# Four graph layers on one core: one-hots of the block build made column by column from one key a lane, and one f32 product for the weights

## The reference, cut to what matters

```python
edge_index = jnp.stack([src, dst])
h = jnp.maximum(_layernorm(x, axis=-1), 0.0)
x = x + _L0_gnn_ref(h, edge_index, ...)                        # message MLP with attention, 2 steps
h = jnp.maximum(_layernorm(x, axis=-1), 0.0)
x = x + _L1_gnn_ref(h, edge_weight, src, dst, ...)             # weighted means both ways, GRU
h = jnp.maximum(_layernorm(x, axis=-1), 0.0)
x = x + _L2_gnn_ref(h, edge_index, edge_attr_4, ...)           # 4 edge types, 4 GRU steps
h = jnp.maximum(_layernorm(x, axis=-1), 0.0)
x = x + _L3_gnn_ref(h, edge_index, edge_type_16, ...)          # 16 relations
```

```python
m = ft[src] * w[:, None]
msum = jax.ops.segment_sum(m, dst, num_segments=n_nodes)
wsum = jax.ops.segment_sum(w, dst, num_segments=n_nodes)
```

## Time and profile before

| | |
|---|---|
| Timed runs | 7994.43 us median of 3 (7987.53 to 8007.56) |
| Profiled execution | 8035.26 us, span of its instructions 8033.2 us |
| PE busy | 5862.3 us, 73% of the span |
| DVE busy | 3623.5 us, 45% |
| ACT busy | 1789.9 us, 22% |
| POOL busy | 2370.6 us, 30% |
| `decode` | from about 579.5 to 597 us |
| `build_blocks` | from about 597 to 1411 us |

### The profile page before, as it was taken

One profiled execution on the slowest core, in us unless ns is written; L12 is line 12 of the kernel. 1 busy time (PEld: TensorE's weight loads), 2 busy tenths in 40 slices (PEclk: granted clock), 3 DMA queues, 4 the chain that ended last, 5 costly groups with the idle time before them and its releaser, 6 DMA issues. The chain is left out here.

```text
span 8033.2 us, 101908 instructions
## 1 busy us (share of the span) xinstructions
PE 5862.3 (73%) x31333; PEld 4116.2 (51%) x31441; DVE 3623.5 (45%) x7508; ACT 1789.9 (22%) x4498; POOL 2370.6 (30%) x2471
## 2 busy tenths in 40 slices
PE   1437777566766676666668989899898997666665
PEld 1334444366666656666664444444444443566555
DVE  6889999355555545555556532221222214111111
ACT  1006666233333333333331010100101002000000
POOL 0000000355655535555550000000000000666665
PEclk8669999788888888888888999999999998555555
DMA  1005555333333423333335635355453543111111
GB/s 50 1 7 212 204 207 207 111 101 100 102 100 100 98 79 101 101 101 101 100 100 184 230 133 192 128 192 176 143 192 127 192 164 136 45 44 45 45 44 43
DMA packets 418900, 951.09 MB, mean 118 GB/s; under 512 B 61905, under 2 KB 274310, under 8 KB 408582
## 3 DMA queue, kind: packets, MB, share of 16 engines
q1 hardware_dynamic: 314502, 681.10, 24.9%
q0 software_dynamic: 104192, 267.02, 12.3%
HBM read 741.69 MB, written 206.20 MB: 118 GB/s over the span
## 5 line engine op out<-in xcount | busy, mean ns | idle before, releaser
L1516 POOL DMA_INDIRECT ring<-rows,stage x1632 | 1586.9, 972 | 2038.4 <-issue 1064.8
L1587 PE MATMUL ps<-here,spread 128*128 x3264 | 1098.7, 467 | 843.2 <-DVE ring L1546 576.8
L1166 PE MATMUL ps<-strip,trans_part 128*128 128x512 f16 (+1 forms) x8400 | 1645.4, 357 | 14.9 <-DVE trans_part L1127 14.9
L1406 POOL DMA_INDIRECT ring<-rows,stage x808 | 772.2, 956 | 2993.9 <-ACT stage L1390 2581.0
L1166 PEld LDWEIGHTS ps<-strip,trans_part 128*128 128x128 bf16 x8400 | 781.1, 98 | 930.6 <-issue 65.7
L1587 PEld LDWEIGHTS ps<-here,spread 128*128 128x128 f32 x3264 | 656.6, 223 | 967.2 <-issue 899.1
L1546 DVE TENSOR_TENSOR ring<-ring,ps 128x512 f32<-128x512 f32 x816 | 560.5, 687 | 1259.7 <-remote 611.3
L1444 PE MATMUL ps<-ring,mark 128*128 128x128 f32 x1616 | 627.0, 488 | 373.2 <-DMA ring<-rows,stage 242.4
L1605 PE MATMUL ps<-ring,mark 128*128 128x128 f32 x3264 | 772.4, 327 | 0.0
L1605 PEld LDWEIGHTS ps<-ring,mark 128*128 128x128 f32 x3264 | 648.9, 221 | 65.1
L1444 PEld LDWEIGHTS ps<-ring,mark 128*128 128x128 f32 x1616 | 433.4, 326 | 397.0 <-issue 397.0
(11 more groups left out here) (288 smaller groups left out, 6279.3 us busy)
## 6 DMA issues: line engine op xcount, KB each, us to landing
strip<-adj SPq DMA_DIRECT2D x400, 800.0 KB, 4.4
adj<-piece SPq DMA_DIRECT2D x125, 640.0 KB, 3.1
locs<-loc_rows SPq DMA_DIRECT2D x420, 128.0 KB
ahead<-ahead_piece SPq DMA_DIRECT2D x125, 320.0 KB, 2.2
back<-back_piece SPq DMA_DIRECT2D x125, 320.0 KB, 2.4
sheet<-ahead SPq DMA_DIRECT2D x25, 1600.0 KB, 8.7
sheet<-back SPq DMA_DIRECT2D x25, 1600.0 KB, 7.2
ring<-rows,stage POOLq DMA_INDIRECT x2440
```

The source lines that it names most:

```text
L1166: last = eng.matmul(k.ps[:, b, 0:cols], part[:, s % TABLES, m, t * D:(t + 1) * D], strip[:, n % RING, c0:c0 + cols], start=n == 0 and m == ...
L1406: eng.indirect_dma_start(ring[:, t, :], None, rows, bass.IndirectOffsetOnAxis(stage[:, t:t + 1], 0)).then_inc(s_full[q], 16)
L1516: eng.indirect_dma_start(ring[:, t, :], None, rows, bass.IndirectOffsetOnAxis(stage[:, t:t + 1], 0)).then_inc(s_full[q], 16)
L1587: last = eng.matmul(hid[:, j, :], spread[:, q, t * P:(t + 1) * P], here[:, bass.ds(cols[t] * 2, W2)], start=True, stop=True)
```

## The change

`decode` stores one number a lane and slot in f32: the new `lane_of` (source lane), `dst_of`, `pair_of`, and `weight_of`, the sum of the three weight parts, made by two additions. `src_of` stays as it was, and feeds `left`.

`build_blocks` makes `left` as before. `right` is made by ten tensor-scalar instructions, one a slot, that compare a row of 512 column numbers (f16) with one key a lane. `down` and `heavy` are f32 now and made slot by slot with 128 columns each: `down` compares with the destination lane, `heavy` compares with the source lane and multiplies by the weight, both read as one operand a lane. The order is `left`, all of `right`, then `down` and `heavy` in turn. TensorE makes the weighted blocks by two f32 products a block, where there were six in bf16. `s_hot` counts three steps a group.

```diff
--- before.py
+++ after.py
@@ -507,16 +507,15 @@
     k.back = nc.dram_tensor("back", [NP + 1, NP], F32, kind="Internal").ap()
     with ExitStack() as own:
 
-        src_of, dst_of = (k.sb(n, [P, BINS * 2, 2], BF16, own) for n in ("src_of", "dst_of"))
-        pair_of = k.sb("pair_of", [P, BINS * 2, 2], F16, own)
-        part_of = k.sb("part_of", [P, 3, BINS * 2, 2], BF16, own)
+        src_of = k.sb("src_of", [P, BINS * 2, 2], BF16, own)
+        lane_of, dst_of, pair_of, weight_of = (k.sb(n, [P, BINS * 2], F32, own) for n in ("lane_of", "dst_of", "pair_of", "weight_of"))
         with ExitStack() as inner:
             binned = k.sb("binned", [P, WORDS, NW, NW, 2], F32, inner)
             with ExitStack() as most:
                 sort_bins(k, most, binned)
-            decode(k, inner, binned, src_of, dst_of, pair_of, part_of)
+            decode(k, inner, binned, src_of, lane_of, dst_of, pair_of, weight_of)
         with ExitStack() as inner:
-            build_blocks(k, inner, src_of, dst_of, pair_of, part_of)
+            build_blocks(k, inner, src_of, lane_of, dst_of, pair_of, weight_of)
     k.edges.close()
     with ExitStack() as own:
         build_any(k, own)
@@ -680,7 +679,7 @@
     k.end_phase()
 
 
-def decode(k, own, binned, src_of, dst_of, pair_of, part_of):
+def decode(k, own, binned, src_of, lane_of, dst_of, pair_of, weight_of):
 
     first, second = (k.sb(n, [P, NW, NW, 2], I32, own) for n in ("first_word", "second_word"))
     whole = k.sb("whole", [P, NW, NW, 2], I32, own)
@@ -696,18 +695,20 @@
             c.step(eng.tensor_copy(flat(second), flat(binned[:, 1, :, :, :])))
             c.step(eng.tensor_scalar(flat(whole), flat(first), 1, None, ALU.arith_shift_right))
             c.step(eng.tensor_copy(src_of[:, :, :], both(whole)))
+            c.step(eng.tensor_copy(lane_of[:, :], flat(whole)))
             c.step(eng.tensor_scalar(flat(whole), flat(second), 1, 8, ALU.bitwise_and, ALU.logical_shift_left))
             c.step(eng.tensor_scalar(flat(first), flat(first), 1, 7, ALU.bitwise_and, ALU.logical_shift_left))
             c.step(eng.tensor_scalar(flat(second), flat(second), 1, None, ALU.arith_shift_right))
-            c.step(eng.tensor_copy(dst_of[:, :, :], both(second)))
+            c.step(eng.tensor_copy(dst_of[:, :], flat(second)))
             c.step(eng.tensor_tensor(flat(whole), flat(whole), flat(first), ALU.add))
-            c.step(eng.tensor_tensor(pair_of[:, :, :], both(whole), both(second), ALU.add))
-            for j in range(3):
-                c.step(eng.tensor_copy(part_of[:, j, :, :], both(binned[:, 2 + j, :, :, :])))
+            c.step(eng.tensor_tensor(pair_of[:, :], flat(whole), flat(second), ALU.add))
+
+            c.step(eng.tensor_tensor(weight_of[:, :], flat(binned[:, 2, :, :, :]), flat(binned[:, 3, :, :, :]), ALU.add))
+            c.step(eng.tensor_tensor(weight_of[:, :], weight_of[:, :], flat(binned[:, 4, :, :, :]), ALU.add))
     k.end_phase()
 
 
-def build_blocks(k, own, src_of, dst_of, pair_of, part_of):
+def build_blocks(k, own, src_of, lane_of, dst_of, pair_of, weight_of):
 
     nc = k.nc
     G = 5
@@ -717,9 +718,9 @@
     lane_no = k.sb("lane_no", [P, P], BF16, own)
     pair_no = k.sb("pair_no", [P, T4 * P], F16, own)
     left = k.sb("left", [P, 2, S, P], BF16, own)
-    down = k.sb("down", [P, 2, S, P], BF16, own)
+    down = k.sb("down", [P, 2, S, P], F32, own)
     right = k.sb("right", [P, 2, S, T4 * P], BF16, own)
-    heavy = k.sb("heavy", [P, 2, 3, S, P], BF16, own)
+    heavy = k.sb("heavy", [P, 2, S, P], F32, own)
     piece = k.sb("piece", [P, PIECES, T4, G * P], F16, own)
     ahead = k.sb("ahead_piece", [P, PIECES, G * P], F32, own)
     back = k.sb("back_piece", [P, PIECES, G * P], F32, own)
@@ -745,14 +746,17 @@
                 if g >= 2:
 
                     eng.wait_ge(s_done, g - 1)
-                of = lambda t, n: t[:, at:at + S, :].unsqueeze(2).to_broadcast([P, S, n // 2, 2])
-                eng.tensor_tensor(in_pairs(left[:, b, :, :]), every(lane_no, S), of(src_of, P), ALU.is_equal).then_inc(s_hot, 1)
-                eng.tensor_tensor(in_pairs(right[:, b, :, :]), every(pair_no, S), of(pair_of, T4 * P), ALU.is_equal).then_inc(s_hot, 1)
-                eng.tensor_tensor(in_pairs(down[:, b, :, :]), every(lane_no, S), of(dst_of, P), ALU.is_equal).then_inc(s_hot, 1)
-                eng.wait_ge(s_hot, g * 6 + 1)
-                for j in range(3):
-                    eng.tensor_tensor(in_pairs(heavy[:, b, j, :, :]), in_pairs(left[:, b, :, :]), of(part_of[:, j, :, :], P),
-                                      ALU.mult).then_inc(s_hot, 1)
+                pairs = src_of[:, at:at + S, :].unsqueeze(2).to_broadcast([P, S, P // 2, 2])
+                key = lambda t, e: t[:, at + e:at + e + 1]
+                lanes = k.tile_no[:, 0:P]
+                eng.tensor_tensor(in_pairs(left[:, b, :, :]), every(lane_no, S), pairs, ALU.is_equal).then_inc(s_hot, 1)
+                for e in range(S):
+                    last = eng.tensor_scalar(right[:, b, e, :], pair_no[:, :], key(pair_of, e), None, ALU.is_equal)
+                last.then_inc(s_hot, 1)
+                for e in range(S):
+                    eng.tensor_scalar(down[:, b, e, :], lanes, key(dst_of, e), None, ALU.is_equal)
+                    last = eng.tensor_scalar(heavy[:, b, e, :], lanes, key(lane_of, e), key(weight_of, e), ALU.is_equal, ALU.mult)
+                last.then_inc(s_hot, 1)
 
         @block.tensor
         def _(eng):
@@ -767,7 +771,7 @@
 
             for g in range(GROUPS):
                 b = g % 2
-                eng.wait_ge(s_hot, g * 6 + 2)
+                eng.wait_ge(s_hot, g * 3 + 2)
                 for i in range(G):
                     n = g * G + i
                     if n >= CNT:
@@ -776,15 +780,14 @@
                         e = 2 * i + half
                         last = eng.matmul(k.ps[:, n % CNT, :], left[:, b, e, :], right[:, b, e, :], start=half == 0, stop=half == 1)
                     last.then_inc(s_mm, 1)
-                eng.wait_ge(s_hot, g * 6 + 6)
+                eng.wait_ge(s_hot, g * 3 + 3)
                 if g:
                     eng.wait_ge(s_aev, g)
                 for i in range(G):
                     for half in range(2):
                         e = 2 * i + half
-                        for j in range(3):
-                            last = eng.matmul(psf[:, AHEAD * BANK + i * P:AHEAD * BANK + (i + 1) * P], heavy[:, b, j, e, :],
-                                              down[:, b, e, :], start=half == 0 and j == 0, stop=half == 1 and j == 2)
+                        last = eng.matmul(psf[:, AHEAD * BANK + i * P:AHEAD * BANK + (i + 1) * P], heavy[:, b, e, :],
+                                          down[:, b, e, :], start=half == 0, stop=half == 1)
                 last.then_inc(s_ahead, 1)
                 eng.wait_ge(s_ahead, g + 1)
                 eng.sem_inc(s_done, 1)
```

## The result

| | before | after |
|---|---|---|
| median of the timed runs | 7998.92 us (7987.53 to 8007.56, 4 runs) | 8181.71 us (8173.07 to 8184.92, 4 runs) |
| ratio, 95% interval | | 1.0227 [1.0214, 1.024] |
| profiled span | 8033.2 us | 8181.6 us |
| one group of the block build | 6.41 us | 7.885 us |
| start of the next stage's DMAs | 1411.69 us | 1594.24 us |

The change is slower by 183 us. The forecast was 8107, with a range of 8080 to 8285. The forecast's own range, 8080 to 8135, does not hold the result; the wider one does, because it was stretched to rivals 2 and 3.

The account below looks back on a forecast made before the run. VectorE was taken to bound the block build; +114.4 us for 125 groups, +0.4 at the stage's end and -2.6 in decode gave +112 on the median 7994.4, so 8107 us, range 8080 to 8285.

Parts of the forecast that it names:

- rival 2: `heavy` in the block build: the second lane operand costs 62 ns more, +78 us, 8185; chance 0.16.
- Rival 3: `right` in the block build: two elements per cycle instead of four, +167 us, 8274; chance 0.12.
- VectorE bounds the stage, and nothing hides its work: Block build: the group's period is VectorE's, 6.41 us before and 7.325 after, +114.4 us over 125 groups.
- `down`, 0.196 us: Block build: ten keyed instructions of 128 columns at 0.196 us, 1.96 us a group, was 0.735.
- `right`, 0.267 us, four elements per cycle: Block build: ten keyed instructions of 512 columns, 133 ns streaming and 133 fixed, 2.67 us a group, was 2.73.
- `heavy`, 0.196 us: Block build: ten instructions with two lane operands at the one-operand price, 1.96 us a group, was 2.205.
- Break-even at 0.189 us for a keyed instruction: Block build: average price at which the 30 keyed instructions cost no more than before; forecast average 0.220 us.
- Rival 1: Block build: keyed instructions' fixed cost is 68 ns, TensorE becomes the bound at 5.9 us a group, 7928 us; chance 0.09.
- TensorE, 2.27 us for the f32 products: Block build: ten f32 products a group take 2.27 us, 0.42 more than before, off the path while VectorE is slower.
- The end of the stage, +0.4 us: Last group of the block build: the f32 products' extra 0.42 us is paid once, after VectorE ends.
- TensorE's serial sum, 5.9 us: Block build: TensorE's products, transposes and waits on its own last product come to 5.9 us a group, under 7.3.
- Decode, -2.6 us: Decode of the sorted edges: fewer or shorter casts and additions save 2.6 us, all on the path.

Follow-up runs that it names:

- the run with halves: The changed kernel with each `right` made by two keyed instructions of 256 columns instead of one of 512: 8336.65 us.
- ScalarE's kernel: The changed kernel with `heavy` one wide f32 instruction and `down` compared in bf16 pairs, then widened to f32 by ScalarE: 7887.1 us.

## Why the prediction was right, point by point

- *The outcome:* slower as forecast, but by 183 us where 112 were forecast. That is rival 2, to which I gave 0.16, and not the forecast, to which I gave 0.52. Bound, sign and the other prices held; the size of one term did not.
- *VectorE bounds the stage, and nothing hides its work:* right. VectorE is busy 100.00 of every 100 us from 600 to 1400 in both traces, halving TensorE's f32 products moved nothing, and every change of VectorE's sum came through: -0.604 us a group gave -73 and -76 us, +1.293 gave +155 (162 in the trace).
- *`down`, 0.196 us:* right, 0.195.
- *`right`, 0.267 us, four elements per cycle:* right, 2.63/10 = 0.263, of which 129 ns are fixed by the run with halves. Rival 3 falls. The Trainium skill, page "VectorE: DVE Perf Modes", in its tier table, says the same, and the trace agrees.
- *`heavy`, 0.196 us:* this is the term that was mis-sized. It costs 0.256, near the upper end of 0.258 that I had worked out as rival 2. I had taken the price of the row with one operand, with the reason that the durations do not say that two reads follow one another. No row had two operands, so that was a guess. The runs show that the prices add up: the constant in place of the weight took 60 ns off each, 0.60 us a group, 75 us of the 183. The sum with it is 0.735 + 2.63 + 4.53 = 7.90 us, against 7.885 measured. Rival 2 would have been 190 us slower than before, 7 more than measured; that its time of 8185 lies within 4 us of the median is in part luck, since the median of the kernel before rose by 4.5 us with the fourth run.
- *Break-even at 0.189 us for a keyed instruction:* the measured mean is (7.885 - 0.735)/30 = 0.238, well above it. Rival 1, with 68 ns fixed, would be true of constants (0.13 us for 128 columns), not of operands a lane.
- *TensorE, 2.27 us for the f32 products:* 2.50 in its row, hidden as forecast. In some groups it is more: in the one from 894.59 us the products take 3.65, at a granted clock of 0.50 (1.2 GHz) from 896 to 899, after TensorE had stood idle for 2.19 us; other groups with the same idle time keep 1.00 (2.4 GHz). Groups like this one bring the mean down to 0.92; it costs nothing while VectorE needs 7.885.
- *The end of the stage, +0.4 us:* too small. There the f32 products are not hidden, and those of the last group met the lower clock: 3.59 us in place of 1.85 before, and the transposes behind them 1.07 in place of 0.74. From the start of these products to the next stage's DMAs it is 13.64 us (1580.60 to 1594.24), where it was 11.42 (1400.27 to 1411.69): +2.2.
- *TensorE's serial sum, 5.9 us:* too large, since durations overlap; it is 5.5. That did not touch the forecast, but made rival 1 and the expectation for ScalarE's kernel too slow.
- *Decode, -2.6 us:* busy time fell from 16.41 to 14.01 us, 2.4 less.
- *The profiled execution against the median:* I took the difference to the median of the timed runs, and that was needed: the spans differ by 148 us, the medians by 183.

## What to carry to other kernels

Price a VectorE instruction that waits for nothing, from start to start, as columns over its rate, plus a fixed part, plus a part for each operand that it reads a lane; here that was 68 ns and 60 ns for each. An operand a lane with a faster element rate pays only while the instruction is long: at 512 16-bit columns the two forms were equal (0.263 against 0.273 us a slot), at 128 f32 columns the wide form was cheaper (0.140 a slot against 0.195 with one operand and 0.256 with two). When a product is to be made of wider numbers, keep the instruction that builds its input wide, and give a plain copy to an idle engine whose work leaves the bounding engine's rows as long as they were. Here that was so of ScalarE, and not of GpSimd. Add up start-to-start times, not durations, before naming the next bound.

## What the runs showed of the hardware that I had not expected

- The fixed cost of a keyed instruction is a sum over its operands: 128 f32 columns take 0.13 us with no operand a lane, 0.195 with one and 0.256 with two, and a second arithmetic operation added nothing that shows.
- A GpSimd multiplication of 1280 bf16 columns takes 2.37 us by its row and stops VectorE for 2.07 to 2.13 us of it, whether VectorE runs the one-tensor or the two-tensor form; one product given to an idle GpSimd made the group longer, from 6.30 to 7.64 us with keyed `right` and from 6.41 to 7.81 with the wide one.
